# Seven buffers for the routers' tiles in the context pass, and the second ternary matrix summed and rounded earlier in it

## The chip, the cores and the metric

The kernel runs on one core of a Trainium2 chip. The metric is the device time of one execution in microseconds (us), taken as the median of several. PE is TensorE (matmuls), DVE is VectorE, ACT is ScalarE, POOL is GpSimd, and SP is SyncE, which here only issues DMAs.

## What is computed

Two rounds of cross-attention, each followed by a feed-forward part, on x of 8 x 512 x 512 in float32. In the reference:

```
x = x + tanh(g_xattn[0]) * L0_xattn(layernorm(x), fside, fside, ctx)
x = x + tanh(g_ffn[0])   * L0_ffn(layernorm(x))
x = x + tanh(g_xattn[1]) * L1_xattn(layernorm(x), ctx, ctx)
x = x + tanh(g_ffn[1])   * L1_ffn(layernorm(x))
```

The context ctx has 8 x 77 rows of 512. Three things are computed from it alone: for L0_xattn a matrix for each batch and head, `W_ep = einsum('bhgd,bhge->bhde', rq, rk)` with rq = ctx Wlq and rk = ctx Wlk; and for L1_xattn the keys and the values. L0_ffn multiplies by two weight matrices w1 and w2 of 2048 x 512 that are first made ternary:

```
scale = 1.0 / clip(mean(abs(w)), 1e-05)
wq    = clip(round(w * scale), -1, 1) / scale
```

## The kernel before

The program is a row of passes, and every engine meets a barrier between two of them. The first is `context_pass`; the attention over the 8 batches follows (`attention_pass`), then the ternary feed-forward part, the second attention, the recurrence and the output.

`context_pass` transposes the 616 context rows in five tiles of 128 (the last 104) and then walks through one list of jobs, `ORDER` (from L160), that PE, ACT and DVE all follow. A job is `("rq", t)`, `("rk", t)` or `("v", t)`: one tile of router queries, router keys or values, 12 matmuls each because every product is made of three terms (`split3`, L101); `("k", i)`: one of eight half tiles of L1's keys, 12 narrower matmuls; `("e", b)`: the routers' tile of batch b, W_ep for all 16 heads. Results rotate through six PSUM banks (`RING = 6`); before a job PE waits until the bank's former result has been taken (`free`, L320).

Who takes a result is fixed. ACT takes rq (once for each batch in the tile, multiplied by a mask) and k; DVE takes rk and v; of an e result ACT copies the diagonal blocks of two heads groups and DVE the other two, into a buffer E that SP then stores in HBM. There are two such buffers, so that ACT and DVE each wait, from batch 2 on, until the store from the same buffer two batches ago has landed:

```
if i >= 2:
    act.wait_ge(s_e[i % 2], 16 * (i // 2))
```

Beside the jobs, two tables called `TODO` say what ACT and DVE do after which job. `high(n)` and `low(n)` split a weight into a high part (ACT) and a low part (DVE). `sums(i, j)` (DVE, L462) adds up the absolute values of quarter j of ternary matrix i, `total(i)` (PE, L331) adds the partitions, `mean(i)` (DVE, four tiny operations from L468) makes the scale, `whole(i, j)` (DVE, L484) scales and rounds quarter j to int8, and `sign(i, j)` (ACT, L392) turns it into bf16 -1, 0 or 1. The last quarter of matrix 1 is done by DVE instead, `clipped(3)` (L478). `next_moments`, `next_shift` (DVE) and `next_rows` (ACT, L397) normalise the first rows of x for the next pass.

SP issues all transfers in the order of its code: the weights, w1 in four quarters, w2 in four quarters of four transfers each (`load_second`, L250; it begins with quarter 3, and then 0, 1, 2), stores of E 0 to 4, loads of x and of fside for the next pass, stores of E 5 to 7, the next Wq, the ternary matrix 0, the values, and at the end the keys and ternary matrix 1.

Of the kernel before, what the change touches and what calls it, by code (L numbers as in the profile page):

```python
# [9 lines left out]
ALU = mybir.AluOpType  # L10
# [3 lines left out]
P = 128  # L14
B = 8
# [133 lines left out]
def context_pass(nc, ctx, Wlq, Wlk, Wk, Wv, bk, bv, w1, w2, wep_s, k1_s, v1_s, t1_s, t2_s, undo_s, next_wq, next_wk, x, f, WA, WB, XROW, FROW, ident, stored):  # L149
# [8 lines left out]
    SLOTS = 6  # L158
    HALF = N // 2
# [7 lines left out]
    with Pass(nc, "ctx") as ps:  # L167
# [12 lines left out]
        ps.sb("gap", [P, 2848])  # L180
# [21 lines left out]
        s_e = [ps.sem(f"e{i}") for i in range(2)]  # L202
        s_store = ps.sem("store")
        s_raw = [[ps.sem(f"raw{i}{j}") for j in range(4)] for i in range(2)]
        s_total, s_steps, s_whole, s_sign, s_clip = (ps.sem(n) for n in ("total", "steps", "whole", "sign", "clip"))
# [13 lines left out]
        def chunk(i):  # L219
            return slice(CHUNK * i, CHUNK * i + CHUNK)  # L220
# [14 lines left out]
        def _(sp):  # L235
# [55 lines left out]
            sp.wait_ge(s_sign, 7)  # L291
            sp.wait_ge(s_clip, 1)
# [15 lines left out]
        @block.tensor
        def _(pe):
            pe.wait_ge(s_ident, 5)  # L310
# [31 lines left out]
            for at, (kind, i) in enumerate(ORDER):  # L342
# [33 lines left out]
                if (kind, i) == ("k", 2):  # L376
                    total(1)

        @block.scalar
        def _(act):  # L380
# [19 lines left out]
            def free_of(name):  # L400
# [4 lines left out]
                elif name == "next_q":  # L405
# [4 lines left out]
                    ("v", 4): [("high", "next_q")], ("k", 3): [("sign", 1, 0)], ("k", 5): [("rows",)],  # L410
                    ("k", 6): [("sign", 1, 1)], ("k", 7): [("sign", 1, 2)]}
# [8 lines left out]
            act.wait_ge(s_ident, 4)  # L420
            for kind, i in ORDER:
# [9 lines left out]
                elif kind == "e":  # L431
                    if i >= 2:
                        act.wait_ge(s_e[i % 2], 16 * (i // 2))
                    act.wait_ge(made["e"], i + 1)
                    for j in range(0, HG, 2):
                        rows = slice(DH * j, DH * j + DH)
                        act.activation(E[i % 2][rows, :, j, :], src[rows, :].rearrange("p (c n) -> p c n", c=C)[:, :, DH * j:DH * j + DH],
                                       ACT.Copy).then_inc(taken["ea"], 1)
# [16 lines left out]
        def _(dve):  # L455
# [48 lines left out]
            dve.wait_ge(s_ident, 4)  # L504
# [6 lines left out]
            def next_shift():  # L511
# [3 lines left out]
            TODO = {("rk", 0): lambda: low("k"), ("rk", 1): lambda: sums(0, 0), ("e", 0): lambda: sums(0, 1),  # L515
                    ("rk", 2): lambda: sums(0, 2), ("e", 1): lambda: sums(0, 3), ("e", 2): lambda: mean(0),
                    ("rk", 3): lambda: whole(0, 0), ("e", 3): lambda: whole(0, 1), ("rk", 4): lambda: low("v"),
                    ("e", 4): lambda: low("next_k"), ("e", 5): lambda: whole(0, 2), ("e", 6): lambda: whole(0, 3),
                    ("e", 7): lambda: sums(1, 0), ("v", 0): lambda: sums(1, 1), ("v", 1): lambda: sums(1, 2),
                    ("v", 2): lambda: sums(1, 3)}  # L520
            for kind, i in ORDER:
# [2284 lines left out]
```

## Time and profile before

| | before |
|---|---|
| median of 3 executions | 2590.65 us |
| lowest, highest | 2589.86, 2596.94 us |
| the profiled execution | 2594.13 us |
| its span in the profile | 2592.3 us |
| mean granted TensorE clock | 0.966 of full speed |
| PE busy | 91% of the span |

The span is the time from the first to the last instruction on the core; 1.83 us of the profiled execution lie outside it. Starts of rows in the trace are counted from the start of the span. Of all this the context pass is the first part only: TensorE begins the attention pass at 102.39 us.

### The profile page before, as it was taken

The numbers are of one execution on the slowest core, as the hardware profiler recorded it, in microseconds if no ns is written. First come the engines' busy times: TensorE is split into PE (matmuls) and PEld (weight loads), VectorE is DVE, ScalarE is ACT, GpSimd is POOL, SyncE is SP. The second block draws the span as 40 slices with busy tenths as digits, with TensorE's granted clock in tenths as the row PEclk, the third lists the DMA queues.
The fourth block names the chain that finished last, engine by engine and source line by source line (L and its number), as shares of the span: only waits on it lengthen the run. The fifth ranks groups of instructions, "written<-read, shape, count | busy, mean of one in ns | idle before, by whom it ended". The sixth has DMA issues, their size and how long they took to land. (4 is left out here: it accounts for less than half of the span.)

```text
span 2592.3 us, 40777 instructions
## 1 busy us (share of the span) xinstructions
PE 2358.8 (91%) x16348; PEld 1551.3 (60%) x16348; DVE 1446.0 (56%) x1748; ACT 1058.5 (41%) x1227; POOL 606.0 (23%) x203
## 2 busy tenths in 40 slices
PE   7889999999999987899999878899868999999989
PEld 6655555555555544444444346666656888888867
DVE  5666556555565545777777567878644222222235
ACT  4445445454454443555554534444423221222223
POOL 0026455445564552000000012323210000000000
PEclk9989999999999988999999978999988999999999
DMA  8601101101010102111110130212322000000046
GB/s 258 217 2 49 45 15 43 39 18 48 10 48 11 42 29 106 50 50 49 49 49 33 42 116 32 95 56 87 105 82 86 33 32 18 30 32 32 17 156 217
DMA packets 102014, 163.73 MB, mean 63 GB/s; under 512 B 16996, under 2 KB 39524, under 8 KB 99102
## 3 DMA queue, kind: packets, MB, share of 16 engines
q1 hardware_dynamic: 95918, 150.82, 17.2%
q10 hardware_dynamic: 6000, 11.54, 1.2%
q8 instruction: 71, 1.16, 0.2%
q14 instruction: 25, 0.20, 0.0%
HBM read 112.63 MB, written 49.71 MB: 63 GB/s over the span
## 5 line engine op out<-in xcount | busy, mean ns | idle before, releaser
L1144 DVE TENSOR_REDUCE att_mx<-att_sn 128x2 f32<-128x1024 f32 x256 | 313.6, 1225 | 164.7 <-PE att_sn L956 161.8
L1056 ACT ACTIVATE att_num<-att_st 128x2048 f32<-128x2048 f32 x128 | 240.6, 1880 | 149.8 <-PE att_st L944 93.5
L869 POOL TENSOR_TENSOR att_es<-att_es,att_num 128x2048 f32<-128x2048 f32 x64 | 294.9, 4608 | 15.1 <-ACT att_num L1056 8.8
L865 POOL TENSOR_TENSOR att_es<-att_num 128x2048 f32<-128x2048 f32 x32 | 146.0, 4561 | 371.2 <-PE att_pj L926 362.2
L2517 ACT ACTIVATE rec_ga<-rec_g,rec_bg 128x512 f32<-128x512 f32 x84 | 57.2, 688 | 307.7 <-PE rec_g L2418 307.7
L2418 PE MATMUL rec_g<-weights_a_h,row_weights_h 128*128 128x512 f32 x384 | 153.2, 399 | 13.6 <-ACT rec_ga L2517 11.1
L2418 PE MATMUL rec_g<-weights_a_l,row_weights_h 128*128 128x512 f32 x384 | 151.9, 395 | 0.0
L2418 PE MATMUL rec_g<-weights_a_h,row_weights_l 128*128 128x512 f32 x384 | 151.6, 395 | 0.0
L956 PE MATMUL att_sn<-att_kh,att_qh 32*128 32x512 f32 x512 | 126.6, 490 | 23.6 <-DVE att_mx L1144 23.6
L1717 DVE TENSOR_TENSOR ffn_hs<-ffn_h,ffn_fb 128x1024 f32<-128x1024 f32 x64 | 78.0, 1219 | 116.7 <-PE ffn_h L1463 109.3
L570 POOL TENSOR_TENSOR ffn_ln_rstd<-ffn_ln_var,ffn_ln_power 128x4 f32<-128x4 f32 x8 | 22.0, 2749 | 482.6 <-DVE ffn_ln_var L591 482.6
L1463 PE MATMUL ffn_h<-ffn_xqt,ffn_w 128*128 128x512 bf16 x512 | 122.0, 381 | 12.9 <-DVE ffn_hs L1717 12.9
L956 PEld LDWEIGHTS att_sn<-att_kh,att_qh 32*128 32x128 f32 x512 | 48.0, 184 | 142.4 <-DVE att_mx L1144 103.4
L2039 POOL TENSOR_TENSOR xat_pr<-xat_e,xat_rd 128x1232 f32<-128x1232 f32 x32 | 73.1, 2285 | 248.6 <-DVE xat_rd L2242 241.7
L919 PE MATMUL att_pj<-att_num,att_v 128*32 128x512 f32 x1024 | 125.0, 608 | 0.9 <-DVE att_rd L1129 0.9
L1476 PE MATMUL ffn_c<-ffn_hs,ffn_dg 32*32 32x512 f32 x3072 | 115.5, 635 | 10.8 <-issue 4.2
L2582 DVE SCALAR_TENSOR_TENSOR rec_ga<-rec_ga,rec_c 128x512 f32<-128x512 f32 x32 | 22.1, 690 | 171.3 <-ACT rec_ga L2517 171.3
L570 POOL TENSOR_TENSOR rec_ln_rstd<-rec_ln_var,rec_ln_power 128x4 f32<-128x4 f32 x7 | 7.5, 1068 | 420.7 <-DVE rec_ln_var L591 420.7
L1605 ACT ACTIVATE ffn_ss<-ffn_c,conv_bias 128x512 f32<-128x512 f32 x128 | 77.5, 693 | 67.5 <-PE ffn_c L1476 62.1
L2159 ACT ACTIVATE xat_pt<-xat_pt 77x512 f32<-77x512 f32 x128 | 73.8, 589 | 74.3 <-PE xat_pt L2099 74.1
L1463 PEld LDWEIGHTS ffn_h<-ffn_xqt,ffn_w 128*128 128x128 bf16 x512 | 46.9, 98 | 83.9 <-issue 20.7
L1511 PE MATMUL ffn_a<-ffn_w,ffn_sq 128*128 128x512 bf16 x352 | 84.8, 391 | 9.5 <-ACT ffn_sq L1627 9.5
(400 smaller groups left out, 5675.8 us busy)
## 6 DMA issues: line engine op xcount, KB each, us to landing
rows<-in_x SPq DMA_DIRECT2D x16, 1024.0 KB, 5.3
rows<-x SPq DMA_DIRECT2D x16, 1024.0 KB, 5.2
rows_b<-in_fside_BxSxS SPq DMA_DIRECT2D x8, 1024.0 KB, 7.8
heads<-att_o SPq DMA_DIRECT2D x32, 256.0 KB, 2.3
weights_b_l<-heads SPq DMA_DIRECT2D x8, 1024.0 KB, 5.2
x<-ffn_xr SPq DMA_DIRECT2D x32, 256.0 KB, 2.1
xat_xr<-x SPq DMA_DIRECT2D x8, 1024.0 KB, 5.0
out_x<-x SPq DMA_DIRECT2D x8, 1024.0 KB, 9.1
```

Of the source, the lines that this page charges most:

```text
L865: pool.tensor_tensor(ES[:], E[0][:], E[1][:], ALU.add).then_inc(s_sum, 1)
L869: pool.tensor_tensor(ES[:], ES[:], E[k][:], ALU.add).then_inc(s_sum, 1)
L919: last = pe.matmul(out[heads(j), :], V[:, k, c * P + DH * j:c * P + DH * j + DH], E[k][:, j, :], start=(k == 0), stop=(k == T - 1))
L956: last = pe.matmul(sn_ps[:, r, :], QT[0][c][own, m // 2 * P:m // 2 * P + P], KT[0][c][own, :], start=True, stop=True)
L1056: act.activation(E[k][:], st_ps[:], ACT.Exp, scale=SCALE).then_inc(s_exp, 1)
L1144: dve.tensor_reduce(MX[c % 2][:, m // 2, 2 * DH * (m % 2):2 * DH * (m % 2) + DH + 1:DH], sn_ps[:], AX, ALU.max, negate=True).then_inc(s_ma ...
L1463: last = pe.matmul(h_ps[:, m, :], W1[:, k, i * P:i * P + P], XQT[:, k, :], start=(k == 0), stop=(k == C - 1))
L1476: last = pe.matmul(c_ps[quarter(m), r, :], DG[quarter(r), 3 * (HG * group + m) + k, :], HS[group % 2][quarter(r), m, k:k + S], start=(k == ...
L1511: last = pe.matmul((a_ps, b_ps)[OUT_BANK[front][t]][:], SQ[:, i, t * P:t * P + P], W2[:, i, :], start=(i == 0), stop=(i == HT - 1))
L1605: act.activation(SS[:, i, :], c_ps[:, r, :], ACT.Silu, bias=CB[:, i:i + 1]).then_inc(s_silu, 1)
L1717: dve.tensor_tensor(HS[group % 2][:, 2 * half:2 * half + 2, 1:S + 1], h_ps[:], FB[:].unsqueeze(1).broadcast_to([P, 2, S]), ALU.mult).then_ ...
L2418: last = pe.matmul(g_ps[m % 2][n][:], W[n][a][:, k, m * P:m * P + P], R[c][:, k, :], start=(part == 0 and k == 0 and i == 0), stop=((part ...
```

## The change

There are seven buffers for the routers' tiles instead of two (`ER = 7`), so that only batch 7 reuses one; an unused stretch of SBUF called `gap` shrinks by as much, so every other buffer keeps its place. GpSimd clears seven buffers instead of two; TensorE no longer waits for the clearing, ACT and DVE do before their first job.

The sums, the mean and the rounding of ternary matrix 1 move forward on DVE: the sums between the routers' jobs, the mean and the rounding beside the values. Its `total` on TensorE moves from behind `("k", 2)` to behind `("v", 1)`. ACT makes all four quarters with `sign` and does so earlier; `clipped` is gone. `next_moments`, `next_shift` and `low("next_q")`, which DVE ran behind all jobs, now stand behind `("v", 3)` and `("v", 4)`, and `next_rows` on ACT stands behind `("k", 4)` instead of `("k", 5)`.

```diff
+    ER = 7
...
-        ps.sb("gap", [P, 2848])
+        E += [ps.sb(f"e{i}", [P, C, HG, DH]) for i in range(2, ER)]
+        ps.sb("gap", [P, 288])
...
             make_identity(pool, ident[:], s_ident)
-            for i in range(2):
+            pool.memset(ones[:], 1.0).then_inc(s_ident, 1)
+            for i in range(ER):
                 pool.memset(E[i][:], 0.0).then_inc(s_ident, 1)
-            pool.memset(ones[:], 1.0).then_inc(s_ident, 1)
...
-            pe.wait_ge(s_ident, 5)
+            pe.wait_ge(s_ident, 3)
...
-                if (kind, i) == ("k", 2):
+                if (kind, i) == ("v", 1):
                     total(1)
...
-                    ("v", 4): [("high", "next_q")], ("k", 3): [("sign", 1, 0)], ("k", 5): [("rows",)],
-                    ("k", 6): [("sign", 1, 1)], ("k", 7): [("sign", 1, 2)]}
+                    ("v", 2): [("sign", 1, 0)], ("v", 3): [("sign", 1, 1)], ("v", 4): [("high", "next_q")],
+                    ("k", 2): [("sign", 1, 2)], ("k", 4): [("rows",)], ("k", 5): [("sign", 1, 3)]}
...
-                    if i >= 2:
-                        act.wait_ge(s_e[i % 2], 16 * (i // 2))
+                    if i >= ER:
+                        act.wait_ge(s_e[i % ER], 16 * (i // ER))
...
-                    ("e", 7): lambda: sums(1, 0), ("v", 0): lambda: sums(1, 1), ("v", 1): lambda: sums(1, 2),
-                    ("v", 2): lambda: sums(1, 3)}
+                    ("e", 2): (lambda: mean(0), lambda: sums(1, 3)),
+                    ("rk", 3): (lambda: whole(0, 0),), ("e", 3): (lambda: whole(0, 1), lambda: sums(1, 0)),
+                    ("rk", 4): (lambda: low("v"),), ("e", 4): (lambda: low("next_k"),),
+                    ("e", 5): (lambda: whole(0, 2), lambda: sums(1, 1)), ("e", 6): (lambda: whole(0, 3),),
+                    ("e", 7): (lambda: sums(1, 2),), ("v", 0): (lambda: mean(1),), ("v", 1): (lambda: whole(1, 0),),
+                    ("v", 2): (lambda: whole(1, 1),), ("v", 3): (lambda: whole(1, 2), lambda: next_moments()),
+                    ("v", 4): (lambda: whole(1, 3), lambda: next_shift(), lambda: low("next_q"))}
...
-            next_moments()
-            mean(1)
-            whole(1, 0)
-            next_shift()
-            low("next_q")
-            for j in range(1, 4):
-                whole(1, j)
-            clipped(3)
```

On DVE before, from the last sum of matrix 0 over the routers' tile 2 (the first two `ctx_e` copies) and tile 3 to `whole(0, 1)`; `ctx_wmean`, `ctx_wscale` and `ctx_undo` are written by `mean(0)`, and `ctx_t` by `whole`:

```order
L462 TENSOR_REDUCE ctx_wsum<-ctx_sw 128x1 [waits ctx_raw03]
L536 COPY ctx_e<-ctx_bank 32x4x32 [waits ctx_made_e,ctx_e0]
L536 COPY ctx_e<-ctx_bank 32x4x32
L468 TENSOR_REDUCE ctx_wmean<-ctx_x 128x1 [waits ctx_total]
L470 TENSOR_SCALAR ctx_wmean<-ctx_wmean 128x1 [waits ctx_steps]
L472 RECIPROCAL ctx_wscale<-ctx_wmean 128x1 [waits ctx_steps]
L473 TENSOR_SCALAR ctx_undo<-ctx_wmean 128x1
L526 COPY ctx_rk<-ctx_bank 128x512 [waits ctx_made_rk,ctx_steps]
L484 TENSOR_SCALAR ctx_t<-ctx_sw,ctx_wscale 128x2048
L536 COPY ctx_e<-ctx_bank 32x4x32 [waits ctx_made_e,ctx_e1]
L536 COPY ctx_e<-ctx_bank 32x4x32
L484 TENSOR_SCALAR ctx_t<-ctx_sw,ctx_wscale 128x2048
```

The same stretch of DVE now, without the sum in front (line numbers differ by a few):

```order
L535 COPY ctx_e<-ctx_bank 32x4x32 [waits ctx_made_e]
L535 COPY ctx_e<-ctx_bank 32x4x32
L469 TENSOR_REDUCE ctx_wmean<-ctx_x 128x1 [waits ctx_total]
L471 TENSOR_SCALAR ctx_wmean<-ctx_wmean 128x1 [waits ctx_steps]
L473 RECIPROCAL ctx_wscale<-ctx_wmean 128x1 [waits ctx_steps]
L474 TENSOR_SCALAR ctx_undo<-ctx_wmean 128x1
L463 TENSOR_REDUCE ctx_wsum<-ctx_sw 128x1 [waits ctx_raw13,ctx_steps]
L525 COPY ctx_rk<-ctx_bank 128x512 [waits ctx_made_rk]
L480 TENSOR_SCALAR ctx_t<-ctx_sw,ctx_wscale 128x2048
L535 COPY ctx_e<-ctx_bank 32x4x32 [waits ctx_made_e]
L535 COPY ctx_e<-ctx_bank 32x4x32
L480 TENSOR_SCALAR ctx_t<-ctx_sw,ctx_wscale 128x2048
```

The copies no longer wait for a store (`ctx_e0`, `ctx_e1`), and a sum of matrix 1 (`ctx_raw13`) stands behind `mean(0)`.

On DVE before, from the last copy of the routers' tile 7 through the tiles of L1's values (`ctx_x<-ctx_bank,ctx_bv`), and the first operation of `next_moments` (`BN_STATS`):

```order
L536 COPY ctx_e<-ctx_bank 32x4x32
L462 TENSOR_REDUCE ctx_wsum<-ctx_sw 128x1 [waits ctx_raw10]
L529 TENSOR_TENSOR ctx_x<-ctx_bank,ctx_bv 128x512 [waits ctx_made_v]
L462 TENSOR_REDUCE ctx_wsum<-ctx_sw 128x1 [waits ctx_raw11]
L529 TENSOR_TENSOR ctx_x<-ctx_bank,ctx_bv 128x512 [waits ctx_made_v]
L462 TENSOR_REDUCE ctx_wsum<-ctx_sw 128x1 [waits ctx_raw12]
L529 TENSOR_TENSOR ctx_x<-ctx_bank,ctx_bv 128x512 [waits ctx_made_v]
L462 TENSOR_REDUCE ctx_wsum<-ctx_sw 128x1 [waits ctx_raw13]
L529 TENSOR_TENSOR ctx_x<-ctx_bank,ctx_bv 128x512 [waits ctx_made_v]
L529 TENSOR_TENSOR ctx_x<-ctx_bank,ctx_bv 104x512 [waits ctx_made_v]
L582 BN_STATS ctx_ln_stats<-rows 128x6 [waits ctx_row]
L582 BN_STATS ctx_ln_stats<-rows 128x6 x3
```

DVE from behind the routers' tile 7 on now, up to the `whole` behind the fourth tile of values:

```order
L463 TENSOR_REDUCE ctx_wsum<-ctx_sw 128x1 [waits ctx_raw12]
L528 TENSOR_TENSOR ctx_x<-ctx_bank,ctx_bv 128x512 [waits ctx_made_v]
L469 TENSOR_REDUCE ctx_wmean<-ctx_x 128x1 [waits ctx_total]
L471 TENSOR_SCALAR ctx_wmean<-ctx_wmean 128x1 [waits ctx_steps]
L473 RECIPROCAL ctx_wscale<-ctx_wmean 128x1 [waits ctx_steps]
L474 TENSOR_SCALAR ctx_undo<-ctx_wmean 128x1
L528 TENSOR_TENSOR ctx_x<-ctx_bank,ctx_bv 128x512 [waits ctx_made_v,ctx_steps]
L480 TENSOR_SCALAR ctx_t<-ctx_sw,ctx_wscale 128x2048 [waits ctx_sign]
L528 TENSOR_TENSOR ctx_x<-ctx_bank,ctx_bv 128x512 [waits ctx_made_v]
L480 TENSOR_SCALAR ctx_t<-ctx_sw,ctx_wscale 128x2048 [waits ctx_sign]
L528 TENSOR_TENSOR ctx_x<-ctx_bank,ctx_bv 128x512 [waits ctx_made_v]
L480 TENSOR_SCALAR ctx_t<-ctx_sw,ctx_wscale 128x2048 [waits ctx_sign]
```

One sum of matrix 1 is left behind tile 7 instead of four, `mean(1)` stands behind the first tile of values, and a `whole` behind each tile from the second on, and `BN_STATS` follows next, before the last tile of values instead of behind it.

At the end of the pass on ACT, before (`weights_a_h` is `high("next_q")`, `ctx_rk` a half tile of keys, L392 a `sign`, L397 `next_rows`):

```order
L383 ACTIVATE weights_a_h<-ctx_rq 128x2048 [waits ctx_w_next_q,ctx_made_v]
L443 ACTIVATE ctx_rk<-ctx_bank,ctx_bk 128x308 [waits ctx_made_e,ctx_made_k] x2
L392 ACTIVATE ctx_sw<-ctx_t 128x2048 [waits ctx_whole]
L443 ACTIVATE ctx_rk<-ctx_bank,ctx_bk 128x308 [waits ctx_made_e,ctx_made_k] x2
L397 ACTIVATE rows<-rows,ctx_shift,ctx_ln_rstd 128x512 [waits ctx_rows]
L397 ACTIVATE rows<-rows,ctx_shift,ctx_ln_rstd 128x512 x3
L443 ACTIVATE ctx_rk<-ctx_bank,ctx_bk 128x308 [waits ctx_made_e,ctx_made_k]
L392 ACTIVATE ctx_sw<-ctx_t 128x2048 [waits ctx_whole]
L443 ACTIVATE ctx_rk<-ctx_bank,ctx_bk 128x308 [waits ctx_made_e,ctx_made_k]
L392 ACTIVATE ctx_sw<-ctx_t 128x2048 [waits ctx_whole]
```

And now, from the last quarters of matrix 0 on (the fourfold row is two quarters of each matrix):

```order
L393 ACTIVATE ctx_sw<-ctx_t 128x2048 [waits ctx_whole] x4
L384 ACTIVATE weights_a_h<-ctx_rq 128x2048 [waits ctx_w_next_q,ctx_made_v]
L444 ACTIVATE ctx_rk<-ctx_bank,ctx_bk 128x308 [waits ctx_made_e,ctx_made_k]
L393 ACTIVATE ctx_sw<-ctx_t 128x2048 [waits ctx_whole]
L444 ACTIVATE ctx_rk<-ctx_bank,ctx_bk 128x308 [waits ctx_made_e,ctx_made_k] x2
L398 ACTIVATE rows<-rows,ctx_shift,ctx_ln_rstd 128x512 [waits ctx_rows]
L398 ACTIVATE rows<-rows,ctx_shift,ctx_ln_rstd 128x512 x3
L444 ACTIVATE ctx_rk<-ctx_bank,ctx_bk 128x308 [waits ctx_made_e,ctx_made_k]
L393 ACTIVATE ctx_sw<-ctx_t 128x2048 [waits ctx_whole]
L444 ACTIVATE ctx_rk<-ctx_bank,ctx_bk 128x308 [waits ctx_made_e,ctx_made_k] x2
```

Two quarters of matrix 1 have gone ahead of the key tiles, and the pass now ends on ACT with two copies of keys instead of a `sign`.

## Rows read from the trace of the kernel before

**Rows 1.** The page of the whole kernel: its span.

```profile
span 2592.3 us, 40777 instructions
```

**Rows 2.** Who waited for whom in 0 to 103 us: total, times, longest.

```profile
ACT ctx_e L437 <- DMA routers<-ctx_e: 22.9, 2, 16.9
```

**Rows 3.** Timeline of DVE: start, duration, instruction, idle before it and its releaser.

```profile
37.56 2.29 DVE L462 TENSOR_REDUCE ctx_wsum<-ctx_sw 128x1 f32<-128x2048 f32 x1
53.25 0.61 DVE L536 COPY ctx_e<-ctx_bank 32x128 f32<-32x128 f32 x2 [13.40 <-DMA routers<-ctx_e]
...
54.53 0.69 DVE L526 COPY ctx_rk<-ctx_bank 128x512 f32<-128x512 f32 x1
55.14 1.28 DVE L484 TENSOR_SCALAR ctx_t<-ctx_sw,ctx_wscale 128x2048 int8<-128x2048 f32 x1
...
59.23 2.29 DVE L458 TENSOR_TENSOR weights_a_l<-rows,weights_a_h 128x2048 fp32r<-128x2048 f32 x1
...
85.78 2.46 DVE L582 BATCH_NORM_STATS2 ctx_ln_stats<-rows 128x6 f32<-128x512 f32 x4
...
89.39 1.28 DVE L484 TENSOR_SCALAR ctx_t<-ctx_sw,ctx_wscale 128x2048 int8<-128x2048 f32 x1
```

**Rows 4.** Timeline of ACT, same columns.

```profile
56.13 1.26 ACT L429 ACTIVATE ctx_rq<-ctx_bank,ctx_masks 104x512 f32<-104x512 f32 x2
57.28 1.91 ACT L383 ACTIVATE weights_a_h<-rows 128x2048 fp32r<-128x2048 f32 x1
...
90.71 1.91 ACT L392 ACTIVATE ctx_sw<-ctx_t 128x2048 bf16<-128x2048 int8 x1 [3.26 <-DVE ctx_t L484]
92.53 0.91 ACT L443 ACTIVATE ctx_rk<-ctx_bank,ctx_bk 128x308 f32<-128x308 f32 x2
93.33 2.92 ACT L397 ACTIVATE rows<-rows,ctx_shift,ctx_ln_rstd 128x512 f32<-128x512 f32 x4
...
98.75 1.91 ACT L392 ACTIVATE ctx_sw<-ctx_t 128x2048 bf16<-128x2048 int8 x1
```

**Rows 5.** Timeline of PE, same columns.

```profile
50.12 0.40 PE L108 MATMUL ctx_bank<-weights_b_h,ctx_xtl 128*104 128x512 f32 x1
55.93 4.74 PE L363 MATMUL ctx_bank<-ctx_rk,ctx_rq 128*128 128x128 f32 x24 [5.42 <-ACT ctx_e L437]
60.43 0.39 PE L108 MATMUL ctx_bank<-ctx_xth,ctx_kh 128*128 128x308 f32 x1
...
63.88 2.84 PE L363 MATMUL ctx_bank<-ctx_rk,ctx_rq 128*128 128x128 f32 x24
66.48 0.48 PE L108 MATMUL ctx_bank<-weights_a_h,ctx_xth 128*128 128x512 f32 x1
...
69.34 0.39 PE L108 MATMUL ctx_bank<-weights_a_h,ctx_xth 128*128 128x512 f32 x1
...
84.72 0.38 PE L331 MATMUL ctx_x<-ctx_wsum,ctx_ones 128*128 128x4 f32 x2 [2.43 <-DVE ctx_wsum L462]
...
102.39 3.67 PE L889 MATMUL att_st<-ident,rows 128*128 128x128 f32 x16 [8.75 <-ACTq L1007]
```

**Rows 6.** PE in stretches: length, busy (matmuls), granted clock, DMA share, GB/s.

```profile
52.00:54.00 2.00, 0.00 (x0) 0.73 0.08 32
...
80.00:84.00 4.00, 2.29 (x15) 1.00 1.00 419
```

**Rows 7.** Loads of w2 (L250): issues, and us from issue to landing.

```profile
L250 SPq DMA_DIRECT2D ctx_sw<-in_L_ffn_w x16: 432/888/2501, 17.4 to 35.4; - x16
...
DMA to landing us min/median/max: 15.5/17.5/19.7
```

**Rows 8.** Timeline of SP's queue, columns as in rows 3.

```profile
100.68 0.33 SPq L293 DMA_DIRECT2D ternary<-ctx_sw  x1
```

**Rows 9.** DMA issues from 100 to 115 us: KB each, median us to landing.

```profile
ternary<-ctx_sw SPq DMA_DIRECT2D x1, 2048.0 KB, 8.1
```

**Rows 10.** PE's first use of the reloaded routers' tiles, timeline as above.

```profile
114.03 1.02 PE L902 MATMUL att_pj<-att_raw,att_wr 128*128 128x512 f32 x2
```

More of the change, by code:

```diff
@@ L201, in context_pass @@
         taken = {n: ps.sem(f"taken_{n}") for n in ("rq", "rk", "v", "ea", "ed", "k")}
-        s_e = [ps.sem(f"e{i}") for i in range(2)]
+        s_e = [ps.sem(f"e{i}") for i in range(ER)]
         s_store = ps.sem("store")
         s_raw = [[ps.sem(f"raw{i}{j}") for j in range(4)] for i in range(2)]
-        s_total, s_steps, s_whole, s_sign, s_clip = (ps.sem(n) for n in ("total", "steps", "whole", "sign", "clip"))
+        s_total, s_steps, s_whole, s_sign = (ps.sem(n) for n in ("total", "steps", "whole", "sign"))
         STEPS_N = 8
@@ L295, in _ @@
             sp.wait_ge(s_store, 16 * (NT + 2))
-            for i in range(2):
-                sp.wait_ge(s_e[i], 16 * B // 2)
+            for i in range(ER):
+                sp.wait_ge(s_e[i], 16 * len(range(i, B, ER)))
         @block.gpsimd
@@ L301, in _ @@
             make_identity(pool, ident[:], s_ident)
-            for i in range(2):
+            pool.memset(ones[:], 1.0).then_inc(s_ident, 1)
+            for i in range(ER):
                 pool.memset(E[i][:], 0.0).then_inc(s_ident, 1)
-            pool.memset(ones[:], 1.0).then_inc(s_ident, 1)
             ln.pool_setup(pool)
@@ L436, in _ @@
                         rows = slice(DH * j, DH * j + DH)
[L437 removed]
+                        act.activation(E[i % ER][rows, :, j, :], src[rows, :].rearrange("p (c n) -> p c n", c=C)[:, :, DH * j:DH * j + DH],
                                        ACT.Copy).then_inc(taken["ea"], 1)
@@ L513, in next_shift @@
                 rows0.inc(dve.scalar_tensor_tensor(shift[:], ln.mv[:, :, 0], -1.0, ln.rstd[:], ALU.mult, ALU.mult))
[L515 to L518, printed above, removed]
-                    ("e", 7): lambda: sums(1, 0), ("v", 0): lambda: sums(1, 1), ("v", 1): lambda: sums(1, 2),
-                    ("v", 2): lambda: sums(1, 3)}
+            TODO = {("rk", 0): (lambda: low("k"),), ("rk", 1): (lambda: sums(0, 0),), ("e", 0): (lambda: sums(0, 1),),
+                    ("rk", 2): (lambda: sums(0, 2),), ("e", 1): (lambda: sums(0, 3),),
+                    ("e", 2): (lambda: mean(0), lambda: sums(1, 3)),
[5 more added lines that the diff above has]
+                    ("v", 4): (lambda: whole(1, 3), lambda: next_shift(), lambda: low("next_q"))}
             for kind, i in ORDER:
@@ L535, in _ @@
                         rows = slice(DH * j, DH * j + DH)
-                        dve.tensor_copy(E[i % 2][rows, :, j, :], src[rows, :].rearrange("p (c n) -> p c n", c=C)[:, :, DH * j:DH * j + DH]
+                        dve.tensor_copy(E[i % ER][rows, :, j, :], src[rows, :].rearrange("p (c n) -> p c n", c=C)[:, :, DH * j:DH * j + DH]
                                         ).then_inc(taken["ed"], 1)
-                if (kind, i) in TODO:
-                    TODO[kind, i]()
-            next_moments()
-            mean(1)
-            whole(1, 0)
-            next_shift()
-            low("next_q")
-            for j in range(1, 4):
-                whole(1, j)
-            clipped(3)
+                for todo in TODO.get((kind, i), ()):
+                    todo()
 class LayerNorm:
```

17 lines of the change are left out of this document (6 added, 11 removed).

## The prediction

> **What bounds the kernel now.** I read the page for the span [rows 1], then the list of waits for the context pass, then the timelines of DVE, ACT and PE beside each other, and last the DMA issues. The change touches only the context pass, and PE opens the next pass at 102.39 us after 8.75 us of idleness that ended on ACT [rows 5]. So the question is how much earlier that instruction can start; everything behind it has the same code.
>
> Two things stretch the pass. First, ACT and DVE stand still for the stores of the routers' tiles: ACT 22.9 us in two waits, the longest 16.9 [rows 2], and DVE 13.40 us in one, up to 53.25 us [rows 3]. The first store is slow because the queue still holds the quarters of w2: their issues run to 35.4 us and each takes up to 19.7 us to land [rows 7], so the last is there at about 35.4 + 17.7 = 53 (the median plus a little). PE goes on while it has banks, until 50.12 + 0.40 = 50.52 us, then waits 5.42 us, and its next 24 matmuls take from 55.93 to 60.43 = 4.50 us where the same 24 take 63.88 to 66.48 = 2.60 us later [rows 5]. Second, the tail: PE is through at 102.39 - 8.75 = 93.64 us, but DVE, which makes the sums of matrix 1 late, holds PE for 2.43 us before 84.72 [rows 5], gets to `whole(1, 0)` at 89.39 [rows 3], and only then ACT begins the first `sign` of matrix 1 at 90.71 and ends the last at 98.75 + 1.91 = 100.66 us [rows 4]. From there to PE's first matmul of the next pass are 1.73 us.
>
> **The change, step by step.** Durations are from rows 3 to 5, given as start to start where a following row allows it: a sum 2.30 us, `low` 2.3, `whole` 1.3, two copies of a routers' tile on DVE 0.65, the four operations of a mean 54.53 - 53.25 - 0.65 = 0.63, a tile of rk or v on DVE 0.61, moments 89.39 - 85.78 - 0.63 = 2.98; on ACT two rq operations 57.28 - 56.13 = 1.15, `high` and `sign` 1.9, a half tile of keys (92.53 to 93.33) 0.40, rows 2.9; on PE a tile of values 69.34 - 66.48 = 2.86 for the first and then about 2.77, two half tiles of keys 63.88 - 60.43 = 3.45. I allow 0.2 us from an engine's end to the start of one that waits for it.
>
> Up to 39.85 us (37.56 + 2.29) nothing moves [rows 3]. With seven buffers DVE then copies tile 2 (to 40.5), makes the mean (41.2) and runs sum 3 of matrix 1 (43.5), whose quarter of w2 was the first issued, at 17.4, and so landed by 20 + 19.7 = 40 at most [rows 7]. Then rk 3, `whole`, tile 3, `whole`, sum 0: 43.5 + 0.6 + 1.3 + 0.65 + 1.3 + 2.3 = 49.65, before rk 4 is made at 50.5. So the two inserted sums lie under PE's work, where DVE stood idle before. ACT: rq 4 is done by about 49.2, `high("v")` to 51.1, `high("next_k")` to 53.0.
>
> DVE from 50.7: rk 4 to 51.3, `low("v")` to 53.6, tile 4 54.3, `low("next_k")` 56.6, tile 5 57.2, `whole` 58.5, sum 1 60.8, tile 6 61.5, `whole` 62.8, tile 7 63.4, sum 2 65.7. PE does not stop at 50.52 us any more: tiles 4 and 5 at full clock 2.60 (to 52.9 from its last issue at 50.3), half keys 3.45 (56.4), tiles 6 and 7 2.60 (59.0), and the values start at 59.0, as `low("v")` is done at 53.6. They started at 66.48 [rows 5], so this place brings 7.5 us: 5.42 of waiting, 1.90 of slow matmuls, 0.2 of restarting.
>
> The new wait is `total(1)` behind the second tile of values. PE is there at 59.0 + 2.86 + 2.77 = 64.6; the last sum ends at 65.7; PE waits about 1.2 us, with the other tiles of values and the keys queued behind it (before: 2.43 us, in the keys). Values 2 to 4 then run from 66.1 to 74.4, six half tiles of keys at 1.72 to 84.7. DVE beside them: v 0 66.2, mean 67.1 (it must wait for `total`), v 1 and `whole` 69.0, v 2 and `whole` 71.1, v 3 (made at 72.0) and `whole` 73.9, moments 76.9, v 4 77.5, `whole` 78.8, shift, `low("next_q")` to 81.2. ACT: the first two `sign` by 73.1, `high("next_q")` 74.8 to 76.7, then half keys, a `sign` to 79.1, half keys to 80.3, rows to 83.2, half keys and the last `sign` to 85.5, two half keys to 86.3. DVE ends 5 us ahead of that, PE 1.6; ACT ends the pass at 86.3 instead of 100.66: 14.4 us earlier. `clipped` costs DVE less and ACT one more `sign` of 1.9, which is in this count.
>
> SP issues the keys' store and that of matrix 1 together behind ACT's end; before, only the latter, an issue of 0.33 us, stood there [rows 8]. I take 0.4 us for it. Five more clearings of 128 x 512 on GpSimd are some 3.5 us, if each takes what DVE takes for a tile of that size (0.69) [rows 3]; ACT and DVE ask for them only before their first job, behind the transposition of the context and the splitting of the first weights, which hides them, and uncovered they would cost those 3.5. GpSimd's one power operation has v 4 and a `whole` beside it. Sum: 14.4 - 0.4 = **14.0 us** less, PE opening the next pass at 88.4.
>
> The profiled execution took 2594.13 us, 3.5 above the median of 2590.65. It would become 2580.1, and the median **2576.7 us**.
>
> **The clock, weighed.** After PE's pause of 5.42 us the granted clock had fallen (0.73 of full speed on average from 52 to 54 us, so from 2.4 down to 1.2 GHz within it) [rows 6], and after the one of 8.75 us PE's first 16 transpositions take 3.67 us [rows 5], also a half-clock rate. A pause of 2.43 us, up to 84.72, left it at 1.00 from 80 to 84 us [rows 6]. Now PE would pause from 84.7 to 88.4, 3.7 us, between the two kinds. I take the fall, as before, so the next pass begins at half clock in both kernels and the sum stays 14.0; if the clock stayed up, the difference between 4.50 and 2.60 us for the same 24 matmuls [rows 5] says some 2 us more, 16.0.
>
> The Trainium skill, "TensorE: Matmul & The Clock Gate", section "The HAM clock gate (the "warmup" mystery)", says that an idle TensorE goes to half clock and must be busy again before it is let up. By that rule the pause between the passes remains a cold start, 14.0; both falls in this trace agree with it, and the short pause shows that not every stop is enough.
>
> **Rivals.** *One, w2 comes too late for its sums.* Sum 0 on DVE needs the second quarter issued. The sixteen issues fill 17.4 to 35.4, so the eighth is at about 26 and lands by 26 + 19.7 = 45.7 [rows 7], 1.7 before its use at 47.4. If instead it came with the last, at 53, everything on DVE behind it would be 5.7 us later, `total(1)` with it, and the gain 8.3 us: 2582.4. The same size would result if ACT and DVE, now nearly without idle time between 50 and 80 us, take 0.1 us more at each of their hand-overs. Chance 0.15, split at the bound of what a measurement can tell.
>
> *Two, the gain is given back behind the barrier.* The stores of the keys and of matrix 1 start together shortly before the next pass, which must reload routers' tiles through the same queue. Matrix 1 alone (2048 KB) took 8.1 us [rows 9]; with the keys (128 x 2464 floats, 1232 KB, at the same rate 4.9) some 13 us of landing from 86.4, to 99.4. PE first used a reloaded tile at 114.03 [rows 10], 11.6 us into its pass, which becomes 100.0. That is close; if each reload is several us later, PE loses 3 to 8 us, leaving 2580 to 2585, and to undo the whole gain the tile would have to land 14 us late, at 114. Against it: before, the two stores overlapped almost as much. Chance 0.07.
>
> *Three, slower.* Moving a pass by 14 us can make PE's clock fall at other pauses of the attention pass, whose code is the same. One us at half clock costs half a us of PE work, so the change turns slower than before by 0.3% when PE spends 2 x (14.0 + 7.8) = 44 us more at 1.2 GHz; it would give 2598 or more. Nothing in the rows speaks for it, and the mean granted clock is 0.966 as it is. Chance 0.03.
>
> *Four, more than 18 us*, with the clock kept up at the barrier and `total(1)` without a wait: 2572 or less. Chance 0.04.
>
> **How the numbers follow.** The forecast, a gain of 10 to 18 us, has 0.71, which with the rivals makes 1. A measurement of this kernel tells about 0.3%, 7.8 us, from no change. Faster than that are the forecast, the fourth, and two thirds of the first (0.71 + 0.04 + 0.10), with a little of the second: 0.87. Within it 0.10, slower 0.03. The range leaves out the third, half of the fourth and the worse half of the second: 2571 to 2583.
>
> **What would show it.** Right: no wait of DVE or ACT on a store before tile 7; PE without a pause between 50 and 56 us, full clock there, the first value matmul near 59.0; a wait of about 1.2 us at `total(1)` near 65; DVE's last `low` near 81, ACT's last keys near 86, PE's first transposition of the next pass near 88.4, and the distance from there to the end unchanged. Wrong: a DMA wait before a sum of matrix 1; the values starting later than 61 us, because `low("v")` is late; the waits moved to `total(1)`, a stop of 4 us or more; ACT ending after 90; or a longer stretch from PE's first use of a reloaded tile on.

## The result, and the profile after

| | before | changed |
|---|---|---|
| median | 2599.11 us (22 executions) | 2586.82 us (22 executions) |
| lowest | 2588.73 us | 2574.93 us |
| profiled execution, its span | 2592.3 us | 2585.2 us |
| mean granted TensorE clock there | 0.966 | 0.962 |
| ratio | | 0.995, interval 0.9937 to 0.9962 |

The ratio is that of the fast executions; one of before's 22 took 2835.52 us. The kernel became 0.5% faster, 9.9 to 16.4 us of 2599. A forecast of 14.0 us less lies in that interval. The time itself, 2586.8 us, lies above the range of 2571 to 2583 us, because the median of before over 22 executions is 8.5 us above the one over three on which the range was set.

DVE in the changed kernel, its timeline (to be held against [rows 3]):

```profile
39.78 0.61 DVE L535 COPY ctx_e<-ctx_bank 32x128 f32<-32x128 f32 x2
...
47.01 2.28 DVE L463 TENSOR_REDUCE ctx_wsum<-ctx_sw 128x1 f32<-128x2048 f32 x1
50.44 0.69 DVE L525 COPY ctx_rk<-ctx_bank 104x512 f32<-104x512 f32 x1 [1.15 <-PE ctx_bank L108]
51.05 2.28 DVE L459 TENSOR_TENSOR weights_a_l<-rows,weights_a_h 128x2048 fp32r<-128x2048 f32 x1
...
63.09 2.29 DVE L463 TENSOR_REDUCE ctx_wsum<-ctx_sw 128x1 f32<-128x2048 f32 x1
...
79.09 0.16 DVE L509 SCALAR_TENSOR_TENSOR ctx_shift<-ctx_ln_mv,ctx_ln_rstd 128x4 f32<-128x4 f32 x1 [0.91 <-POOL ctx_ln_rstd L561]
79.17 2.29 DVE L459 TENSOR_TENSOR weights_a_l<-ctx_rq,weights_a_h 128x2048 fp32r<-128x2048 f32 x1
```

The copies of tile 2 come straight behind the sum, where 13.40 us of waiting stood. The last of the sums ends at 63.09 + 2.29 = 65.38, and everything of DVE at 81.46.

The end of ACT's work in the pass, and PE at the same places as in [rows 5]:

```profile
83.00 1.90 ACT L393 ACTIVATE ctx_sw<-ctx_t 128x2048 bf16<-128x2048 int8 x1
84.81 0.90 ACT L444 ACTIVATE ctx_rk<-ctx_bank,ctx_bk 128x308 f32<-128x308 f32 x2
```

```profile
50.24 2.84 PE L364 MATMUL ctx_bank<-ctx_rk,ctx_rq 128*128 128x128 f32 x24
...
58.89 0.48 PE L108 MATMUL ctx_bank<-weights_a_h,ctx_xth 128*128 128x512 f32 x1
...
65.43 0.39 PE L332 MATMUL ctx_x<-ctx_wsum,ctx_ones 128*128 128x4 f32 x2 [0.75 <-DVE ctx_wsum L463]
...
88.09 3.68 PE L880 MATMUL att_st<-ident,rows 128*128 128x128 f32 x16 [3.71 <-ACTq L998]
```

PE runs on at 50 us without a pause, starts the values at 58.89 where it was 66.48, stops 0.75 us for the total and begins the next pass at 88.09 where it was 102.39: 14.3 us earlier. The clock, in stretches of PE (length, busy, matmuls, granted clock, then DMA):

```profile
50.00:56.00 6.00, 6.00 (x48) 1.00 0.76 250
...
86.00:88.00 2.00, 0.00 (x0) 0.70 0.75 315
88.00:90.00 2.00, 1.91 (x9) 0.50 1.07 446
```

It is full from 50 to 56 us, where it had fallen before, and half at the start of the next pass, as before: it falls inside the pause of 3.71 us.

Yet the span is shorter by only 7.1 us. The passes can be cut where GpSimd begins its first clearing of each (recurrence and output taken together). All profiles of this study side by side, in us:

| profile | context | attention | ternary | second attention | rest | span |
|---|---|---|---|---|---|---|
| before | 102.33 | 895.87 | 530.02 | 407.51 | 656.57 | 2592.3 |
| before_again | 102.19 | 903.80 | 530.23 | 405.55 | 656.43 | 2598.2 |
| changed | 88.03 | 901.36 | 530.48 | 408.65 | 656.68 | 2585.2 |
| changed_again | 88.58 | 901.57 | 532.42 | 410.23 | 656.70 | 2589.5 |
| changed_third | 88.40 | 901.70 | 529.89 | 406.48 | 656.23 | 2582.7 |
| changed_fourth | 88.42 | 901.70 | 529.89 | 405.94 | 656.55 | 2582.5 |
| buffers_alone | 90.33 | 900.65 | 533.20 | 406.36 | 656.56 | 2587.1 |
| moves_alone | 104.78 | 893.15 | 530.26 | 405.49 | 656.52 | 2590.2 |
| three_buffers | 97.79 | 900.44 | 532.44 | 410.63 | 656.20 | 2597.5 |
| four_buffers | 88.39 | 905.64 | 530.37 | 408.70 | 656.70 | 2589.8 |
| shorter_tail | 87.20 | 903.66 | 531.53 | 408.10 | 656.21 | 2586.7 |
| kept_busy | 88.07 | 891.21 | 530.28 | 405.42 | 656.52 | 2571.5 |
| kept_busy_again | 88.48 | 891.60 | 530.35 | 405.42 | 656.45 | 2572.3 |
| tail_and_busy | 87.43 | 893.39 | 532.90 | 406.47 | 656.41 | 2576.6 |
| pause_added | 101.33 | 906.84 | 532.37 | 410.13 | 656.73 | 2607.4 |
| before_busy | 102.66 | 901.03 | 532.73 | 410.27 | 656.71 | 2603.4 |

The context pass repeats within 0.6 us for one kernel. The attention pass does not always: 895.87 and 903.80 us for the same code of before, while the four profiles of the changed kernel lie at 901.36 to 901.70.

### The profile page after: what moved, and what is told of

Same layout as the page of the kernel before. It is cut to its first block and busy times, and to the rows that moved or that the text cites. A ratio compares the mean times of both kernels' runs of the same rounds, so it can differ in the third digit from the quotient of the medians.

```text
span 2585.2 us, 40732 instructions
## 1 busy us (share of the span) xinstructions
PE 2362.0 (91%) x16307; PEld 1554.4 (60%) x16348; DVE 1443.2 (56%) x1747; ACT 1060.5 (41%) x1228; POOL 608.7 (24%) x208
## 5 line engine op out<-in xcount | busy, mean ns | idle before, releaser
L2409 PE MATMUL rec_g<-weights_a_h,row_weights_h 128*128 128x512 f32 x384 | 152.9, 398 | 13.6 <-ACT rec_ga L2508 11.1
L1454 PE MATMUL ffn_h<-ffn_xqt,ffn_w 128*128 128x512 bf16 x486 | 117.0, 383 | 16.4 <-DVE ffn_hs L1708 12.9
L2090 PEld LDWEIGHTS xat_pt<-xat_ident,xat_pr 128*77 128x77 f32 x512 | 67.1, 161 | 48.5 <-issue 23.4
```

The lines of the kernel that those rows point to most:

```text
L1454: last = pe.matmul(h_ps[:, m, :], W1[:, k, i * P:i * P + P], XQT[:, k, :], start=(k == 0), stop=(k == C - 1))
L2409: last = pe.matmul(g_ps[m % 2][n][:], W[n][a][:, k, m * P:m * P + P], R[c][:, k, :], start=(part == 0 and k == 0 and i == 0), stop=((part ...
```

## The experiments

Five single executions above 2650 us, four of before and one of four_buffers, are left out of all means below. Behind the context pass all these kernels have the same code.

**The same kernels again.** No edit.

> The changed kernel once more, unaltered. Theory: the change takes 14.3 us out of the context pass, always, and what comes behind it varies from one execution to the next with TensorE's granted clock, so this profile shows the next pass beginning at 88.0 us again (within 0.2), while the attention pass takes anything between 893 and 903 us. Rival: moving the pass forward costs the attention pass something (901.4 us in the first profile of the changed kernel against 895.9 before), so it takes 900 us or more here too.

> The kernel before once more, unaltered. Theory: the next pass begins at 102.3 us again (within 0.2), the attention pass takes anything between 893 and 903 us, and the times scatter by some 15 us about 2598, so that a median of three executions can be 8 us off. Rival (the attention pass is longer only with the change): 896 us here, within 1.

Measured: changed_again 88.58 and 901.57 us, median 2587.9 of 9, ratio 0.9938 (0.9915 to 0.996). before_again 102.19 and 903.80 us, median 2599.11 of 12, from 2587.66 to 2608.21, ratio 0.9986 (0.9967 to 1.0005). So the context pass repeats, if a little less closely than 0.2 us, and an attention pass of over 900 us comes without the change too. Over all 47 executions of the changed kernel in the study the mean is 2584.8 us, over 131 of before 2599.4 us (standard deviations 5.4 and 5.8): 14.6 us apart, with a standard error of 0.9. The context pass gives 13.6 to 14.3 of it (102.19 and 102.33 against 88.03 to 88.58), so the change costs the later passes at most some 2 us; a cost of over 5 us, which the rival read from the first two profiles, falls. The scatter goes with the clock: over the changed kernel's first 22 executions 0.001 of mean granted clock less is 1.85 us more, and that line holds 0.84 of their variance.

Where it comes from is seen by laying the clock of two profiles side by side. In the changed kernel's, 127 us into the attention pass, first PE's timeline, then its stretches:

```profile
215.52 0.50 PE L947 MATMUL att_sn<-att_kh,att_qh 32*128 32x512 f32 x2 [1.61 <-DVE att_mx L1135]
```

```profile
214.00:216.00 2.00, 0.48 (x8) 1.00 0.00 0
216.00:218.00 2.00, 2.00 (x20) 0.63 0.00 0
218.00:220.00 2.00, 2.00 (x6) 0.50 0.00 0
220.00:222.00 2.00, 2.00 (x5) 0.50 0.00 0
```

And the corresponding place of kept_busy (below), where the same pause comes 3 us earlier:

```profile
212.47 0.50 PE L950 MATMUL att_sn<-att_kh,att_qh 32*128 32x512 f32 x2 [1.62 <-DVE att_mx L1138]
```

```profile
210.04:212.04 2.00, 0.82 (x8) 1.00 0.00 0
212.04:214.04 2.00, 1.57 (x19) 1.00 0.00 0
214.04:216.04 2.00, 2.00 (x9) 1.00 0.00 0
216.04:218.04 2.00, 2.00 (x17) 1.00 0.00 0
```

The same pause of 1.6 us, for the same maximum, is followed by half clock (1.2 GHz) in one and by full clock (2.4 GHz) in the other. That this does not take two programs is seen in kept_busy_again, the same program as kept_busy, where the clock falls behind this pause:

```profile
213.08 0.50 PE L950 MATMUL att_sn<-att_kh,att_qh 32*128 32x512 f32 x2 [1.62 <-DVE att_mx L1138]
```

```profile
213.00:214.00 1.00, 0.92 (x16) 0.93 0.00 0
214.00:215.00 1.00, 1.00 (x11) 0.50 0.00 0
```

Such falls go with the differences in the attention column. Added up from the granted clock in stretches of 1 us, TensorE spent 45.1 and 66.7 us of that pass at half clock in the two profiles of before, 39.0 and 38.6 in those of kept_busy and kept_busy_again, and 64.7 in each of the changed kernel's four; over all 16 profiles 1 us more of it goes with 0.44 us more of the pass, and the relation holds 0.91 of their variance. The falls are thus the likely cause of these differences, though no run changes them alone. Nor are they spread at random: in all four profiles of the changed kernel they begin at the same nine places, within 1 us (0, 33, 57, 128, 238, 818, 835, 848 and 889 us into the pass).

**Buffers alone.** The kernel before with `ER = 7` and all that belongs to it:

```diff
+    ER = 7
...
-                    if i >= 2:
-                        dve.wait_ge(s_e[i % 2], 16 * (i // 2))
+                    if i >= ER:
+                        dve.wait_ge(s_e[i % ER], 16 * (i // ER))
```

> Seven buffers, the work on matrix 1 where it was before. Theory, worked out with the durations of the trace: no wait on a store, values from 58.9 us on, but the four sums beside the values, moments, mean, rounding and sign behind them again; ACT ends near 89.4 and the next pass begins near 91.1, so the buffers alone bring 11.2 of the 14.3 us. Rival: without the moves DVE and ACT hold the end at about the distance behind the values that it had before (the pass ended 35.8 us behind the first matmul of the values, now 58.9 + 35.8 = 94.7), so the buffers alone bring 7.6.

Measured: the next pass at 90.33 us, so 12.0 of 14.3 us; median 2587.47 of 9, ratio 0.9945 (0.9927 to 0.9963). The last of ACT and PE's start:

```profile
86.56 1.90 ACT L394 ACTIVATE ctx_sw<-ctx_t 128x2048 bf16<-128x2048 int8 x1
```

```profile
90.39 3.68 PE L891 MATMUL att_st<-ident,rows 128*128 128x128 f32 x16 [7.09 <-ACTq L1009]
```

ACT ends at 88.46, not 89.4; the rival's 94.7 is refuted. The pass still ends on ACT, long behind the matmuls: PE pauses 7.09 us, so the moves are what shortens this tail further.

**Moves alone.** The changed kernel with `ER = 2` and the old `gap`:

```diff
-    ER = 7
+    ER = 2
...
-        ps.sb("gap", [P, 288])
+        ps.sb("gap", [P, 2848])
```

> The work on matrix 1 moved as in the change, with two buffers. Theory: DVE and ACT wait until 53.2 us as before, and as three of the sums stand in the program behind that wait, DVE has 7 us more to do before the values; TensorE is held at the total behind the second tile of values until about 78; the next pass begins near 100, a gain of some 2 us at most. Rival: the two parts add up, so this brings what the buffers alone leave of the 14.3 us, 3 to 7 us.

Measured: 104.78 us, 2.5 us later than before; median 2592.49 of 12, ratio 0.999 (0.9968 to 1.0011). DVE, then PE:

```profile
53.24 0.61 DVE L535 COPY ctx_e<-ctx_bank 32x128 f32<-32x128 f32 x2 [12.78 <-DMA routers<-ctx_e]
...
77.17 0.61 DVE L535 COPY ctx_e<-ctx_bank 32x128 f32<-32x128 f32 x2 [2.41 <-DMA routers<-ctx_e]
77.81 2.29 DVE L463 TENSOR_REDUCE ctx_wsum<-ctx_sw 128x1 f32<-128x2048 f32 x1
```

```profile
80.16 0.59 PE L332 MATMUL ctx_x<-ctx_wsum,ctx_ones 128*128 128x4 f32 x2 [6.43 <-DVE ctx_wsum L463]
```

Neither side had the sign right. The last sum stands behind tile 7, which waits 2.41 us for a store, and PE, held 6.43 us at the total in the middle of the values, loses more than the shorter tail brings. In the context pass the parts do not add up: alone they bring 12.0 and -2.5 us, together 14.3.

**Three and four buffers.** The same edit with `ER = 3` and `ER = 4`.

> The changed kernel with four buffers for the routers' tiles instead of seven. Theory: the first store lands near 53.2, when the loads of w2 are through, and tile 4 is due at 52.4 on ACT and 53.4 on DVE, so four buffers cost 0.8 us at that place at most, later ones are free in time, and the next pass begins between 88.0 and 88.8. Rival: the stores of tiles 2 and 3 land so late behind the loads of x and fside that tiles 6 and 7 wait for them, and the pass ends some us later, 90 or more.

> The changed kernel with three buffers. Theory: tile 3 is now the first that needs a store landed (53.2 us), due at 44.9, so ACT and DVE stop for 8 us at tile 3, as long as TensorE has banks it goes on, the values begin some 5 to 7 us later, and the next pass begins near 94, between the changed kernel and the two buffers (104.8). Rival: DVE has 1.2 us of slack at tile 4 and two sums that could run in the stop only if they stood ahead of it; as they stand behind it, the whole 8 us are lost and it begins near 96 to 98.

Measured: four begin the next pass at 88.39 us, within what the changed kernel itself shows (88.03 to 88.58), three at 97.79; ratios 0.9953 (0.9931 to 0.9974) and 0.9957 (0.9939 to 0.9975). ACT at its tile 4 with four buffers, ACT at its tile 3 with three, and PE's total with three:

```profile
53.07 0.56 ACT L438 ACTIVATE ctx_e<-ctx_bank 32x128 f32<-32x128 f32 x2
```

```profile
53.47 0.56 ACT L438 ACTIVATE ctx_e<-ctx_bank 32x128 f32<-32x128 f32 x2 [11.13 <-DMA routers<-ctx_e]
```

```profile
72.62 0.59 PE L332 MATMUL ctx_x<-ctx_wsum,ctx_ones 128*128 128x4 f32 x2 [5.39 <-DVE ctx_wsum L463]
```

With four nothing waits for a store. With three the rival is nearer (97.79 against 96 to 98): the sums that could fill the 7.19 us that DVE waits before tile 3 stand behind it.

The times of the variants that keep a wait do not follow the context column. three_buffers has a mean of 2589.8 us (12, standard error 1.8), 9.6 below before's where its context pass gives 4.5; moves_alone has 2596.6 (12, standard error 2.0), 2.8 below before's where its pass is 2.5 longer. So what is said of both is shown for the context pass alone, and why the whole kernel takes less than that pass says is open.

**A pause at the end.** Seven ACT copies behind the pass's last work:

```diff
+            act.wait_ge(s_lo, step("next_q"))
+            for n in range(7):
+                act.activation(RQS[:, 0:C, :], RQS[:, 0:C, :], ACT.Copy).then_inc(s_pause, 1)
+                act.wait_ge(s_pause, n + 1)
```

> The changed kernel with seven more ACT copies of 128x2048 behind its last work in the context pass, each waiting for the one before, about 14 us (they rewrite a buffer that nobody reads again in that pass). Theory (the gain lies in the context pass alone, and what follows does not care when it starts): the next pass begins near 102.5 us, the rest is as in every other profile, and the ratio to before is 1.000 within its interval. Rival (the later passes are a few us longer with the changed kernel, for its code or its order): slower than before, 1.001 to 1.003, with an attention pass of 901 us or more.

Measured: 101.33 us, mean 2597.9 of 12, ratio 0.9999 (0.9976 to 1.0022). With 13.3 us of pause the whole gain is gone, within an interval of some 6 us either way, as it must be if the gain is the context pass. Its profile had an attention pass of 906.84 us, the longest of all, as the rival said; its times give no sign of the rival, but the interval does not exclude the lower part of its 1.001 to 1.003.

**The clock held up at the barrier.** Eight matmuls whose result nobody reads, behind PE's last keys; in before_busy thirty of them in the kernel before:

```diff
+            pe.wait_ge(s_steps, 2 * STEPS_N)
+            for _ in range(8):
+                pe.matmul(x_ps[0].rearrange("p c n -> p (c n)"), XT[0][:, 0, 0:P], WB[0][:, 0, :], start=True, stop=True)
```

> The changed kernel with eight more matmuls of 128x512 (into a bank that is read by nobody any more) behind TensorE's last keys, so that its pause before the next pass shrinks from 3.7 to under 2 us. Theory, by the clock term of the prediction: the granted clock stays at 2.4 GHz over the pause, the first 16 transpositions take 2.5 us and not 3.68, and DVE's first maximum comes some 13.5 us behind the start of the pass, not 15.5; 2 us in all, too little for the times. Rival: the clock falls all the same, or the first transpositions wait for their copies on ACT and DVE and not for the clock, and the distance stays 15.5.

PE's start of the attention pass in kept_busy, and DVE's first maximum there and in the changed kernel:

```profile
88.14 1.97 PE L883 MATMUL att_st<-ident,rows 128*128 128x128 f32 x16 [1.84 <-ACTq L1001]
```

```profile
101.88 1.23 DVE L1138 TENSOR_REDUCE att_mx<-att_sn 128x2 f32<-128x1024 f32 x1 [1.33 <-PE att_sn L950]
```

```profile
103.63 1.23 DVE L1135 TENSOR_REDUCE att_mx<-att_sn 128x2 f32<-128x1024 f32 x1 [1.33 <-PE att_sn L947]
```

The 16 transpositions take 1.97 us and not 3.68, and from the start of the pass to the maximum are 13.74 us, not 15.54: the 1.8 us expected. But the times fell further, to a median of 2578.04 of 12, so it was run again, and the same done to before.

> The kernel with the eight idle matmuls once more, unaltered: its first 12 runs had a median of 2578.0 us where the changed kernel has 2587, more than the 1.7 us seen at the start of the pass. Theory (chance): the times fall in groups, by whether TensorE's clock falls at a few pauses of 1.6 us in the attention pass, and the median comes out between 2575 and 2588 here, with a mean of 2582 to 2584. Rival (holding the clock up at the barrier also makes later falls rarer): median 2576 to 2580 again.

> The changed kernel a third time, beside the two others on one chip: the next pass at 88.0 to 88.6 us, mean of the runs 2585, ratio to before 0.994 to 0.996. A single clock fall in the attention pass more or less than in the earlier profiles moves the span by about 3 to 5 us.

> The kernel before with thirty idle matmuls of 128x512 behind TensorE's last keys, so that its pause of 8.75 us before the next pass shrinks to under 2. Theory (a clock held up at the start of the attention pass is worth more than the 1.7 us seen there, because it also sets at which later pauses the clock falls): the next pass begins at 102.3 us, its 16 transpositions take 1.97 us, the attention pass takes 890 to 894 us as in the three profiles with the clock held up, and the mean of the runs is 5 to 8 us below before's, near 2592. Rival (only the first 1.7 us): mean 2596 to 2598, attention pass anywhere between 892 and 905 us.

> The changed kernel a fourth time, as the neighbour of the other on one chip: mean of the runs near 2585, attention pass near 901.5 us as in its three earlier profiles (901.4, 901.6, 901.7) and the clock fall 136 us into it again. If that pass comes out near 892 instead, the fall there is a matter of chance for this kernel too.

Measured: kept_busy_again a median of 2575.28 of 6, ratio 0.9912 (0.989 to 0.9935), attention pass 891.60 us; changed_third 2584.11, ratio 0.9941 (0.9918 to 0.9963); changed_fourth 2583.81, ratio 0.9941 (0.9919 to 0.9962). The median of kept_busy_again lies just inside the range given for chance and below the rival's; its mean of 2576.7 us lies below the 2582 to 2584 given for chance. In changed_fourth the clock fell again in the middle of the attention pass as in the three profiles before it, 128 us into the pass by the stretches of 1 us and not 136. All 18 executions of kept_busy and kept_busy_again have a mean of 2579.0 us, 5.8 below the changed kernel's 47, with a standard error of 1.5, so more than the 1.8 us at the place, against my expectation of chance. before_busy also begins its pass with full clock, but its attention pass took 901.03 us, its mean is 2596.6 us (12), 2.8 us below before's with a standard error of 2.0, ratio 0.9981 (0.9962 to 1.0): there the rival holds, 1.7 us and little else. So a held clock at the start does not in general prevent later falls. Where the rest of the 5.8 us is can be seen in part: in the two profiles with the eight matmuls several of the later falls are shorter or missing, and the attention pass is 10 us shorter. But these two profiles are of the fastest and the second fastest execution of their runs, and the changed kernel too has executions as short, 7 of 47 under 2576 us, against 7 of 18 here. Why such executions are more frequent stays open.

**A shorter tail.** The last quarter by DVE again, one sum earlier; and both edits together.

```diff
-                    ("k", 2): [("sign", 1, 2)], ("k", 4): [("rows",)], ("k", 5): [("sign", 1, 3)]}
+                    ("k", 2): [("sign", 1, 2)], ("k", 4): [("rows",)], }
...
-                    ("e", 5): (lambda: whole(0, 2), lambda: sums(1, 1)), ("e", 6): (lambda: whole(0, 3),),
-                    ("e", 7): (lambda: sums(1, 2),), ("v", 0): (lambda: mean(1),), ("v", 1): (lambda: whole(1, 0),),
+                    ("e", 5): (lambda: whole(0, 2), lambda: sums(1, 1)), ("e", 6): (lambda: whole(0, 3), lambda: sums(1, 2)),
+                    ("v", 0): (lambda: mean(1),), ("v", 1): (lambda: whole(1, 0),),
...
-                    ("v", 4): (lambda: whole(1, 3), lambda: next_shift(), lambda: low("next_q"))}
+                    ("v", 4): (lambda: whole(1, 3), lambda: next_shift(), lambda: low("next_q"),
+                                lambda: clipped(3))}
```

> The changed kernel with the last quarter of matrix 1 made by DVE (clip) behind everything else, as before, and the third remaining sum ahead of the last routers' tile instead of behind it. Theory: the wait at the total behind the second tile of values (0.75 us) goes nearly away, TensorE ends 0.6 us earlier, ACT loses a sign of 1.9 us at the end and now ends with TensorE's last keys, near 84.4, and the next pass begins near 86.6, 1.4 us earlier than with the change; the times can't show it (ratio to before 0.994). Rival: the clip on DVE (1.2 us behind a low that ends at 81.5) or the later copy of the last routers' tile takes the place of what was removed, and the next pass begins at 88.0 or later.

> The shorter tail and the eight idle matmuls together. Theory: the two parts touch different waits, so the next pass begins near 86.6 us and its DVE maximum comes 13.8 us later, 3 us ahead of the changed kernel in all; the mean of the runs is some 3 us below the changed kernel's, which can be told only if the clock's falls are as frequent in both. Rival: with TensorE's last keys now nearly the last work of the pass, the eight matmuls (1.9 us) hold the barrier, and the next pass begins near 87.2.

ACT's last work in shorter_tail, and PE's start of the next pass:

```profile
84.34 0.52 ACT L445 ACTIVATE ctx_rk<-ctx_bank,ctx_bk 128x308 f32<-128x308 f32 x1 [0.91 <-PE ctx_bank L108]
```

```profile
87.27 2.89 PE L887 MATMUL att_st<-ident,rows 128*128 128x128 f32 x16 [2.96 <-ACTq L1005]
```

The pass ends at 87.20 us, 0.8 to 1.4 earlier than in the four profiles of the changed kernel and 0.6 later than expected, and ACT now waits for PE: the end has passed to the matmuls. Median 2582.37 of 12, ratio 0.9943 (0.9922 to 0.9965). Both together: 87.43 us, as that rival said, median 2581.35 of 6, ratio 0.9932 (0.9907 to 0.9956). By its times the best kernel run is the changed one with the eight matmuls (mean 2579.0 us of 18); the one with both edits (2581.7 of 6, standard error 1.9) is not told apart from it.

## Why the prediction was right in its steps and wrong in its range

- **The first stretch.** The pause at 50 us, its slow matmuls and its restart were to bring 7.5 us, the values to start at 59.0. They start at 58.89.
- **The sums under PE's work.** Right: all four run without a DMA wait; the last ended at 65.38, forecast 65.7. Rival one, w2 too late, did not occur.
- **The new wait.** 1.2 us forecast, 0.75 measured. That it was placed with so little slack is what moves_alone and three_buffers show: 6.43 and 5.39 us at the same instruction.
- **What was not read.** The prediction names one wait of DVE on a store, 13.40 us. There was a second, before tile 7:

```profile
73.23 0.61 DVE L536 COPY ctx_e<-ctx_bank 32x128 f32<-32x128 f32 x2 [4.82 <-DMA routers<-ctx_e]
```

  The sum did not need it, as it was built from the new order and not from what was taken away. The row from 80 to 84 us, cited for the clock behind the pause that ends at 84.72, ends before that pause does; the trace bears the reading out all the same, at 1.00 from 84 to 97 us. And five more clearings on GpSimd took 2.3 us, not 3.5 (seven 3.32, two 0.99); they hid as forecast, since tile 2 is copied at 39.78 us, right behind the sum.
- **The tail.** DVE's end at 81.2, measured 81.46, with a wait of 0.91 us on GpSimd that I had not seen, and that nothing depends on; ACT's end at 86.3, measured 85.71.
- **Barrier.** I allowed 1.73 + 0.4 us from ACT's end; measured 88.09 - 85.71 = 2.38. That 0.25 more and the 0.6 less of the tail partly cancel.
- **The clock between the passes.** It fell, as taken; kept_busy shows what it is worth at the place, 1.8 us where I had said some 2.
- **Rivals two to four.** The first maximum comes 15.54 us behind the start of the pass, 15.36 before, so the reloads hold nothing back; with the clock held up it is 13.74 us in kept_busy and 13.75 in before_busy. DVE's timeline of before has it here:

```profile
117.75 1.23 DVE L1144 TENSOR_REDUCE att_mx<-att_sn 128x2 f32<-128x1024 f32 x1 [1.34 <-PE att_sn L956]
```

  A slower kernel and one 18 us faster did not come.
- **The sum.** 14.0 us forecast; 14.3 in the first two profiles, 13.6 to 14.3 over all of both kernels, 14.6 between the means of 47 and 131 executions.
- **The step that failed** is the last: "The profiled execution took 2594.13 us, 3.5 above the median of 2590.65. It would become 2580.1, and the median 2576.7 us". It took the median of three executions for the kernel's level. Executions of before run from 2587 to 2609 us with a mean of 2599.4, and three with a median of 2590.65 are three from the lower part. 2599.11 - 14.0 = 2585.1, against 2586.82 measured. The range held only the unknown costs of the change and nothing for this scatter, though the three times shown were already 7 us apart and the text itself named the clock's falls in the attention pass, as the means of a slower kernel only.

## What to carry to other kernels

Find the buffer count from the time of one landing, not from the count of tiles: here the first store, issued behind the loads of w2, landed only at 53 us (16.6 to 16.7 us after its issue, where the quickest of the eight took 2.0 to 2.3), and as many buffers as there are tiles due before that time, four, were enough. Work moved ahead of a wait pays, work moved behind one becomes late for whoever waits for it, so a reordering that shortens its pass with the wait removed can lengthen it with the wait in place. And give the range of a forecast the scatter of the kernel itself: three executions do not fix a level that varies by 20 us.

## What was not expected of the hardware

The same pause of TensorE, 1.6 us at the same instruction, was followed by a fall to half clock in one execution of a program (kept_busy_again) and not in another (kept_busy). The attention pass of before took 895.87 us with 45.1 us at half clock and 903.80 with 66.7. A pause of 3.7 us between the passes came with a fall in each profile of the changed kernel, and one of 1.84 us in its place did not. With pauses of 2.96 us (shorter_tail) and 3.56 us (three_buffers) the clock was still full when TensorE began again and fell about 1 us later.
